# The state-space loop of a decoder kernel: one product with B in each pair of states moved from VectorE to GpSimd, by way of a copy made by ScalarE

## The chip, the cores and the metric

The kernel runs on one core of one Trainium2 chip. The metric is the device time of one execution in microseconds (us), as the median of several executions. Everything is computed in one launch: two decoder layers, six stages one after the other. The change touches one stage, the fourth.

## The reference

The reference is a two-layer decoder on 1024 tokens of width 128. The part that matters is the mixer of the second layer, a selective state-space scan over 1024 tokens with 256 channels (`Din`) and N = 16 states:

```python
dbc = u @ x_proj_w
dt, Bm, Cm = dbc[..., :dt_rank], dbc[..., dt_rank:dt_rank + N], dbc[..., dt_rank + N:]
delta = jax.nn.softplus(dt @ dt_proj_w + dt_proj_b)
A = -jnp.exp(A_log)
dA = jnp.exp(delta[..., None] * A)
dBu = delta[..., None] * Bm[:, :, None, :] * u[..., None]
def step(h, xs):
    dA_t, dBu_t, C_t = xs
    h = dA_t * h + dBu_t
    y = jnp.einsum('bdn,bn->bd', h, C_t)
    return (h, y)
```

So for each state n and each channel: a decay `exp(-a*delta)`, a drive `du * B[n]` with `du = delta * u`, a scan over the tokens, and a read `h * C[n]` that is summed over the states.

## The kernel before

The stages run one after the other; between two stages all engines meet and GpSimd clears the semaphores of the stage that ended (line 2807). The state-space stage is `mamba_stage`. Channels lie on the 128 partitions in two halves (`CH` = 2, index `j`), tokens along the free dimension, so that every large tile is 128x1024 float32. After a preparation that computes `delta` and `du`, each engine runs its own loop over pairs of states, `Fori(0, STATES // 2) as m`, with `s` = 0, 1 for the two states of a pair and `j` = 0, 1 for the two halves: 16 states, 32 (state, half) steps. There is no planner; the order on each engine is the order of its program, and semaphores join them.

- **ScalarE** (lines 1693 to 1701): for each (s, j) it waits until the scan before it is done (`scanned`) and writes the decay into the PSUM tile `B[1]` (line 1697). There is only one decay tile. After both halves it waits for TensorE's `c_mm` and copies the row of C, spread over all partitions, from `B[0]` into `c_rows[s]` (line 1701).
- **TensorE** (lines 1749 to 1788): `spread` multiplies with selector matrices so that one row of B or C stands on all 128 partitions, always in the PSUM tile `B[0]`; two matmuls of 512 columns. `B[0]` serves B and C in turn: the row of C is spread when both drives of the state are done (`spread_c`, line 1766 waits on `driven`), and the next row of B when C has been copied out (`spread_b`, line 1770 waits on `c_copied`). `add_reads` (eight matmul records in a row) adds the two read products of a state into `B[2]` and `B[3]`. In `next_state(n)` the order is: C of state n + 1, B of state n + 2, reads of state n.
- **VectorE** (lines 1872 to 1882): for each (s, j) the drive `du * B[0]` into the tile `drive[:, j, :]` (line 1877), and then the scan, which reads the decay in `B[1]` and the drive (line 1881).
- **GpSimd** (lines 1648 to 1655): the read product `state * c_rows` of each (s, j) (line 1654), after `c_copied` and the scan.

The four lines of VectorE that set the pattern:

```python
V.tensor_tensor(drive[:, j, :], du[:, j, :], B[0][:], ALU.mult).then_inc(S["driven"], 1)
e.wait_ge(S["driven"], 4 * m + (2 * s + j + 1 + DRIVEN0))
e.wait_ge(S["decayed"], 4 * m + (2 * s + j + 1))
V.tensor_tensor_scan(state[:, s, j, :], B[1][:], drive[:, j, :], 0.0, ALU.mult, ALU.add)
```

After the loop VectorE adds the skip term when all reads are summed (`y_all`), gates, and TensorE makes the output projection.

## Time and profile before

| what | value |
|---|---|
| median of 3 runs | 2874.75 us (2874.26 to 2877.35) |
| the profiled execution, its own time | 2881.46 us |
| its span, first to last instruction | 2879.5 us |
| busy over the span: PE, DVE, ACT, POOL | 84%, 75%, 53%, 11% |
| mean granted TensorE clock | 0.906 |
| the loop of the state-space stage, first to last scan | 1453.72 to 1569.72 us |

PE is TensorE, DVE VectorE, ACT ScalarE, POOL GpSimd, SP the queue of SyncE. The page divides the span into slices and gives for each engine the busy share; the loop lies in slices 21 and 22 of 40, the only ones behind the first stage in which GpSimd is much used. The shares of the whole span say little about one loop of 116 us: the timeline of that stretch, in which every instruction has its start, its length, and what ended the idle time before it, says which engine waits for which. In a timeline neighbouring instructions of one form are merged (x2, x8), and the idle time in brackets is that of the engine before the row.

### The profile page before, as it was taken

The page shows a single profiled execution, that of the slowest core. Times are in us where ns is not written, and L with a number is a line of the kernel's source. Part 1 is how long each engine was busy: PE and PEld are TensorE (multiplying, and loading weights), DVE is VectorE, ACT ScalarE, POOL GpSimd, SP SyncE. Part 2 cuts the span into 40 slices and gives each one's busy share as a digit, 9 for nine tenths or more (in the row PEclk, how much of TensorE's full clock was granted, in tenths as well). Part 3 has the DMA queues.
Part 4 walks back from the last instruction along what each step waited for, and adds up shares of the span by engine and source line. Part 5 has one row for each costly group of instructions (what it writes and reads, how often), then busy time and mean ns, then how long its engine had stood idle before and what let it go on. Part 6 is the DMA issues. An engine that isn't in the chain of part 4 may idle for free. (4 is left out here: it accounts for less than half of the span.)

```text
span 2879.5 us, 35672 instructions
## 1 busy us (share of the span) xinstructions
PE 2431.1 (84%) x10344; PEld 894.0 (31%) x10344; DVE 2149.5 (75%) x3171; ACT 1538.8 (53%) x1852; POOL 327.6 (11%) x333
## 2 busy tenths in 40 slices
PE   5888725799999987999657479999999999995997
PEld 3555401122222213444212213333333333332443
DVE  6777748899999204444498689999999999966665
ACT  4544417576767872333343457666676666652111
POOL 5655620000000000000045000000000000000000
PEclk8988855799999997999879679999999999997999
DMA  3433469100000105777200522013013110112000
GB/s 95 135 113 120 141 119 119 26 27 24 24 24 24 30 25 136 192 191 190 56 1 0 125 57 61 28 43 88 26 32 98 31 30 28 32 35 101 0 0 7
DMA packets 186315, 189.65 MB, mean 66 GB/s; under 512 B 18542, under 2 KB 158259, under 8 KB 184909
## 3 DMA queue, kind: packets, MB, share of 16 engines
...
## 5 line engine op out<-in xcount | busy, mean ns | idle before, releaser
L2459 DVE TENSOR_TENSOR y_acc<-y_acc,y_probs 128x1024 f32<-128x1024 f32 x408 | 496.7, 1217 | 33.9 <-ACT y_probs L2155 23.7
L2155 ACT ACTIVATE y_probs<-y_E,y_mask_bias 128x1024 f32<-128x1024 f32 x416 | 441.5, 1112 | 67.6 <-PE y_E L2240 59.2
L1080 ACT ACTIVATE x_probs<-x_E 128x1024 f32<-128x1024 f32 x408 | 397.2, 1023 | 138.0 <-PE x_E L1137 135.6
L1245 DVE TENSOR_REDUCE x_maxima<-x_M 128x1 f32<-128x496 f32 x676 | 420.5, 669 | 26.7 <-PE x_M L1119 15.4
L2249 PE MATMUL y_O<-y_probs,y_values 128*64 128x512 f32 x1664 | 402.8, 605 | 0.0
L2239 PE MATMUL y_E<-y_qa,y_ks 128*128 128x512 f16 x832 | 319.9, 385 | 1.2 <-ACT y_copied L2131 1.2
L2240 PE MATMUL y_E<-y_qb,y_ks 66*128 66x512 f16 x832 | 318.3, 383 | 0.0
L2131 ACT ACTIVATE y_copied<-y_M 128x1024 bf16<-128x1024 f32 x164 | 168.1, 1025 | 209.5 <-PE y_M L2206 209.5
L2397 DVE TENSOR_REDUCE y_maxima<-y_M 128x2 f32<-128x1024 f32 (+1 forms) x195 | 239.0, 1225 | 37.2 <-PE y_M L2206 25.2
L1566 DVE TENSOR_TENSOR f_hidden<-f_act_out,f_spread 128x512 f32<-128x512 f32 x160 | 110.6, 692 | 171.2 <-ACT f_act_out L1450 163.3
L1137 PE MATMUL x_E<-x_qs,x_keys 128*128 128x512 bf16 x816 | 220.8, 385 | 4.6 <-ACT x_probs L1080 2.9
L1150 PE MATMUL x_O<-x_probs,x_values 128*32 128x512 f32 x1632 | 218.0, 606 | 0.6 <-ACT x_probs L1080 0.6
L1450 ACT ACTIVATE f_act_out<-f_b 128x512 f32<-128x512 f32 x160 | 95.5, 598 | 186.6 <-PE f_b L1482 186.6
L2206 PE MATMUL y_M<-y_ks,y_qa 64*128 64x512 f16 x742 | 148.9, 398 | 26.4 <-DVE y_maxima L2397 23.6
L1487 PE MATMUL f_b<-f_hidden,f_weights 128*128 128x512 f32 x320 | 165.0, 598 | 5.3 <-DVE f_hidden L1566 5.3
L1482 PE MATMUL f_b<-f_xnT,f_weights 128*128 128x512 f32 x320 | 165.7, 600 | 1.1 <-ACT f_act_out L1450 1.1
L1119 PE MATMUL x_M<-x_keys,x_qs 64*128 64x496 bf16 x338 | 136.7, 404 | 23.8 <-DVE x_maxima L1245 23.4
L2249 PEld LDWEIGHTS y_O<-y_probs,y_values 128*64 128x64 f32 x1664 | 101.7, 136 | 171.8 <-issue 156.2
L2665 PE MATMUL g_b<-g_w_in,g_xT 128*128 128x512 f32 x256 | 119.6, 609 | 23.7 <-ACT g_xT L2625 16.4
L1119 PE MATMUL x_M<-x_keys,x_qm 64*128 64x496 bf16 x338 | 136.8, 405 | 0.0
L2408 DVE TENSOR_TENSOR y_running<-y_running,y_copied 128x1024 bf16<-128x1024 bf16 x192 | 131.7, 686 | 3.9 <-ACT y_copied L2131 3.4
L2239 PEld LDWEIGHTS y_E<-y_qa,y_ks 128*128 128x128 f16 x832 | 81.6, 98 | 141.6 <-issue 45.8
...
## 6 DMA issues: line engine op xcount, KB each, us to landing
...
```

Of the source, the lines that this page charges most:

```text
L1080: nc.scalar.activation(probs[:, n % 2, 2 * g:2 * g + 2, :], psE[:, 2 * g:2 * g + 2, :], ACT.Exp).then_inc(exped, 1)
L1119: T.matmul(banks[j], q, ks[r, 4 * (u // 2) + 2 * h + j, CHUNK0 * c:CHUNK0 * c + CHUNK0], start=True, stop=True).then_inc(done, 1)
L1137: ins = T.matmul(psE[:, j, :], ks[:, 4 * (u // 2) + j, P * t:P * t + P], qs[:, u, j, :], start=True, stop=True)
L1150: ins = T.matmul(psO[32 * j:32 * j + 32, :], values[:, i, 32 * j:32 * j + 32], probs[:, n % 2, j, :], start=(t == 0), stop=(t == TILES0 - ...
L1245: V.tensor_reduce(maxima[:, 2 * h + j, qt, c:c + 1], psM[(2 * entry + j) % 3][:, 0:CHUNK0], AX.X, ALU.max).then_inc(max_done, 1)
L2131: A(out, scores, ACT.Copy).then_inc(S["spare_copied"], 1)
L2155: A(probs[:, i, :], psE[:, 2 * (i % 2):2 * (i % 2) + 2, :].rearrange("p a b -> p (a b)"), ACT.Exp, bias=mask_bias[:, bass.ds(c * TILES_IN_ ...
L2239: T.matmul(psE[:, 2 * slot + j, :], ks1[:, u // 2 % 2, keys], qa[:, u, j, :], start=True, stop=False)
L2240: ins = T.matmul(psE[:, 2 * slot + j, :], ks2[:, u // 2 % 2, keys], qb[:, u, j, :], start=False, stop=True)
L2249: ins = T.matmul(psO[u % 2][DH1 * j:DH1 * j + DH1, :], values[:, i, DH1 * j:DH1 * j + DH1], probs[:, i, 512 * j:512 * j + 512], start=Fals ...
L2397: V.tensor_reduce(maxima[:, u % 2, :, 2 * g, bass.ds(c, 1)], psO_pair[:] if (u, g) == (0, 1) else psM[:], AX.X, ALU.max)\
L2459: ins = V.tensor_tensor(acc[:, u % 2, :], acc[:, u % 2, :], probs[:, i, :], ALU.add)
```

## The change

GpSimd makes the drive of (s, j) = (1, 1), one of the four of a pair of states, in a tile `pool_drive`; VectorE makes the other three. GpSimd reads B from a new tile `b_rows` in SBUF, which ScalarE copies from `B[0]` once in each pair, at the start of s = 1 and ahead of the decays of that state. GpSimd makes its product between the reads (0, 0) and (0, 1). VectorE's drive (1, 0), which reads `B[0]` as the copy does, waits for `b_copied`. TensorE's `spread_c` counts three drives in a pair, and for s = 1 it waits for the one drive that VectorE makes of that state and for `b_copied`. There are two new semaphores. In full:

```diff
--- before.py
+++ after.py
@@ -1612,10 +1612,11 @@
         drive = sb("drive", [P, CH, TOKENS])
         state, read = sb("state", [P, 2, CH, TOKENS]), sb("read", [P, 2, CH, TOKENS])
         c_rows = sb("c_rows", [P, 2, TOKENS])
+        b_rows, pool_drive = sb("b_rows", [P, TOKENS]), sb("pool_drive", [P, TOKENS])
 
         names = ("load load_in load_sel consts dve to_pow from_pow scaled_in bias_mm biased xn tr xT xz copied conv_done "
                  "silu_done dbc_mm dbc_done reduced split stacked dt_mm z_done neg exped one lned inved soft driver a_exp "
-                 "a_done b_mm c_mm c_copied decayed driven scanned was_read y_mm y_all gated out_mm added").split()
+                 "a_done b_copied pool_driven b_mm c_mm c_copied decayed driven scanned was_read y_mm y_all gated out_mm added").split()
         S = {n: sem(n) for n in names}
         LOADS_IN, LOADS = 3, 8
 
@@ -1647,8 +1648,13 @@
                 nc.gpsimd.memset(upad[:, :, 0:TAPS - 1], 0.0).then_inc(S["consts"], 1)
                 with e.Fori(0, STATES // 2) as m:
                     for s in range(2):
-                        e.wait_ge(S["c_copied"], 2 * m + (s + 1 + C0))
                         for j in range(CH):
+                            if (s, j) == (0, 1):
+                                e.wait_ge(S["b_copied"], m + 1)
+                                e.wait_ge(S["scanned"], 4 * m + SCAN0)
+                                nc.gpsimd.tensor_tensor(pool_drive[:], du[:, 1, :], b_rows[:], ALU.mult)\
+                                    .then_inc(S["pool_driven"], 1)
+                            e.wait_ge(S["c_copied"], 2 * m + (s + 1 + C0))
                             e.wait_ge(S["scanned"], 4 * m + (2 * s + j + 1 + SCAN0))
                             e.wait_ge(S["y_mm"], 4 * m + (2 * s + j - 3 + Y0))
                             nc.gpsimd.tensor_tensor(read[:, s, j, :], state[:, s, j, :], c_rows[:, s, :], ALU.mult)\
@@ -1690,8 +1696,13 @@
                     A(du[:, j, :], delta[:, j, :], ACT.Exp, scale=-1.0).then_inc(S["inved"], 1)
                 e.wait_ge(S["soft"], CH)
                 e.sem_inc(S["c_copied"], C0)
+                e.sem_inc(S["pool_driven"], DRIVEN0)
                 with e.Fori(0, STATES // 2) as m:
                     for s in range(2):
+                        if s == 1:
+                            e.wait_ge(S["b_mm"], 2 * m + 2)
+                            e.wait_ge(S["pool_driven"], m + DRIVEN0)
+                            A(b_rows[:], B[0][:], ACT.Copy).then_inc(S["b_copied"], 1)
                         for j in range(CH):
                             e.wait_ge(S["scanned"], 4 * m + (2 * s + j + SCAN0))
                             A(B[1][:], delta[:, j, :], ACT.Exp,
@@ -1762,28 +1773,30 @@
                                            skip_group_check=True)
                         ins.then_inc(S["y_all"] if last else S["y_mm"], 1)
 
-                def spread_c(n):
-                    e.wait_ge(S["driven"], 2 * n + (2 + DRIVEN0))
-                    spread(0, n + STATES).then_inc(S["c_mm"], 1)
+                def spread_c(m, s):
+                    e.wait_ge(S["driven"], 3 * m + (2 + s))
+                    if s:
+                        e.wait_ge(S["b_copied"], m + 1)
+                    spread(0, 2 * m + (s + STATES)).then_inc(S["c_mm"], 1)
 
                 def spread_b(n):
                     e.wait_ge(S["c_copied"], n + C0)
                     spread(0, n).then_inc(S["b_mm"], 1)
 
-                def next_state(n, s, first=False):
-                    spread_c(n + 1)
-                    spread_b(n + 2)
-                    add_reads(n, s, first)
+                def next_state(m, s, first=False):
+                    spread_c(m if s == 0 else m + 1, 1 - s)
+                    spread_b(2 * m + (s + 2))
+                    add_reads(2 * m + s, s, first)
 
                 spread(0, 0).then_inc(S["b_mm"], 1)
-                spread_c(0)
+                spread_c(0, 0)
                 spread_b(1)
                 next_state(0, 0, first=True)
-                next_state(1, 1)
+                next_state(0, 1)
                 with e.Fori(1, STATES // 2 - 1) as m:
                     for s in range(2):
-                        next_state(2 * m + s, s)
-                spread_c(STATES - 1)
+                        next_state(m, s)
+                spread_c(STATES // 2 - 1, 1)
                 add_reads(STATES - 2, 0)
                 add_reads(STATES - 1, 1, last=True)
                 for h in range(2):
@@ -1798,7 +1811,7 @@
             def _(e):
                 V = nc.vector
                 step = Steps(e, S["dve"])
-                for name, start in (("driven", DRIVEN0), ("was_read", READ0), ("y_mm", Y0), ("scanned", SCAN0)):
+                for name, start in (("was_read", READ0), ("y_mm", Y0), ("scanned", SCAN0)):
                     e.sem_inc(S[name], start)
                 norm_statistics(nc, step, x, stats, moments, 1e-5, var[:]).then_inc(S["to_pow"], 1)
                 V.tensor_scalar(neg_ident[:], ident[0:PROJ, 0:PROJ], -1.0, None, ALU.mult)
@@ -1873,12 +1886,18 @@
                     for s in range(2):
                         e.wait_ge(S["b_mm"], 2 * m + (s + 1))
                         for j in range(CH):
+                            source = pool_drive[:] if (s, j) == (1, 1) else drive[:, j, :]
                             e.wait_ge(S["scanned"], 4 * m + (2 * s + j - 1 + SCAN0))
-                            V.tensor_tensor(drive[:, j, :], du[:, j, :], B[0][:], ALU.mult).then_inc(S["driven"], 1)
-                            e.wait_ge(S["driven"], 4 * m + (2 * s + j + 1 + DRIVEN0))
+                            if (s, j) == (1, 1):
+                                e.wait_ge(S["pool_driven"], m + (1 + DRIVEN0))
+                            else:
+                                if s:
+                                    e.wait_ge(S["b_copied"], m + 1)
+                                V.tensor_tensor(source, du[:, j, :], B[0][:], ALU.mult).then_inc(S["driven"], 1)
+                                e.wait_ge(S["driven"], 3 * m + (2 * s + j + 1))
                             e.wait_ge(S["decayed"], 4 * m + (2 * s + j + 1))
                             e.wait_ge(S["was_read"], 4 * m + (2 * s + j - 3 + READ0))
-                            V.tensor_tensor_scan(state[:, s, j, :], B[1][:], drive[:, j, :], 0.0, ALU.mult,
+                            V.tensor_tensor_scan(state[:, s, j, :], B[1][:], source, 0.0, ALU.mult,
                                                  ALU.add).then_inc(S["scanned"], 1)
                 for j in range(CH):
                     e.wait_ge(S["y_all"], j + 1)
```

## Rows read from the trace of the kernel before

**Rows 1.** Groups, state-space loop and end: line, form, count; busy us, mean ns; idle, releasers.

```profile
L1654 POOL TENSOR_TENSOR ssm_read<-ssm_state,ssm_c_rows 128x1024 f32<-128x1024 f32 x32 | 74.6, 2355 | 94.9 <-ACT ssm_c_rows L1701 91.4 <-DVE ssm_state L1881 3.5
L1881 DVE TENSOR_TENSOR_SCAN ssm_state<-m_b,ssm_drive 128x1024 f32<-128x1024 f32 x32 | 73.3, 2291 | 4.2 <-DVE ssm_drive L1877 3.6
...
L1877 DVE TENSOR_TENSOR ssm_drive<-ssm_du,m_b 128x1024 f32<-128x1024 f32 x31 | 37.5, 1208 | 4.7 <-PE m_b L1752 4.2
L1697 ACT ACTIVATE m_b<-ssm_delta,ssm_a_neg 128x1024 f32<-128x1024 f32 x31 | 34.7, 1120 | 56.1 <-DVE ssm_state L1881 56.1
...
L1701 ACT ACTIVATE ssm_c_rows<-m_b 128x1024 f32<-128x1024 f32 x16 | 16.4, 1025 | 11.8 <-PE m_b L1752 11.8
```

**Rows 2.** First and last scan of the loop, timeline: start us, length us, instruction.

```profile
1453.72 2.29 DVE L1881 TENSOR_TENSOR_SCAN ssm_state<-m_b,ssm_drive 128x1024 f32<-128x1024 f32 x1
...
1569.72 2.29 DVE L1881 TENSOR_TENSOR_SCAN ssm_state<-m_b,ssm_drive 128x1024 f32<-128x1024 f32 x1 [0.23 <-DVE ssm_drive L1877]
```

**Rows 3.** Timeline, all engines, 1485 to 1493 us (x2, x8: merged instructions).

```profile
1485.12 2.29 DVE L1881 TENSOR_TENSOR_SCAN ssm_state<-m_b,ssm_drive 128x1024 f32<-128x1024 f32 x1
...
1487.33 1.20 DVE L1877 TENSOR_TENSOR ssm_drive<-ssm_du,m_b 128x1024 f32<-128x1024 f32 x1
...
1487.55 1.12 ACT L1697 ACTIVATE m_b<-ssm_delta,ssm_a_neg 128x1024 f32<-128x1024 f32 x1 [3.06 <-DVE ssm_state L1881]
...
1488.68 0.60 PE L1752 MATMUL m_b<-ssm_stack,ssm_sel 120*128 120x512 bf16 x2 [0.26 <-DVE ssm_drive L1877]
1488.75 2.29 DVE L1881 TENSOR_TENSOR_SCAN ssm_state<-m_b,ssm_drive 128x1024 f32<-128x1024 f32 x1 [0.23 <-DVE ssm_drive L1877]
1489.32 1.02 ACT L1701 ACTIVATE ssm_c_rows<-m_b 128x1024 f32<-128x1024 f32 x1 [0.66 <-PE m_b L1752]
...
1490.50 0.60 PE L1752 MATMUL m_b<-ssm_stack,ssm_sel 120*128 120x512 bf16 x2 [1.21 <-ACT ssm_c_rows L1701]
1490.59 4.66 POOL L1654 TENSOR_TENSOR ssm_read<-ssm_state,ssm_c_rows 128x1024 f32<-128x1024 f32 x2 [3.17 <-ACT ssm_c_rows L1701]
...
1491.14 1.22 DVE L1877 TENSOR_TENSOR ssm_drive<-ssm_du,m_b 128x1024 f32<-128x1024 f32 x1
1491.17 1.12 ACT L1697 ACTIVATE m_b<-ssm_delta,ssm_a_neg 128x1024 f32<-128x1024 f32 x1 [0.82 <-DVE ssm_state L1881]
...
1492.39 2.29 DVE L1881 TENSOR_TENSOR_SCAN ssm_state<-m_b,ssm_drive 128x1024 f32<-128x1024 f32 x1
```

**Rows 4.** Timeline, the first change of state, 1457 to 1462 us.

```profile
1457.36 2.29 DVE L1881 TENSOR_TENSOR_SCAN ssm_state<-m_b,ssm_drive 128x1024 f32<-128x1024 f32 x1 [0.24 <-DVE ssm_drive L1877]
1458.25 1.02 ACT L1701 ACTIVATE ssm_c_rows<-m_b 128x1024 f32<-128x1024 f32 x1 [0.98 <-PE m_b L1752]
...
1459.33 1.04 PE L1752 MATMUL m_b<-ssm_stack,ssm_sel 120*128 120x512 bf16 x2 [1.12 <-ACT ssm_c_rows L1701]
...
1460.41 1.22 DVE L1877 TENSOR_TENSOR ssm_drive<-ssm_du,m_b 128x1024 f32<-128x1024 f32 x1 [0.75 <-PE m_b L1752]
1461.66 2.29 DVE L1881 TENSOR_TENSOR_SCAN ssm_state<-m_b,ssm_drive 128x1024 f32<-128x1024 f32 x1
```

**Rows 5.** Timeline, two scans with a turn of the loop between them.

```profile
1496.02 2.29 DVE L1881 TENSOR_TENSOR_SCAN ssm_state<-m_b,ssm_drive 128x1024 f32<-128x1024 f32 x1 [0.23 <-DVE ssm_drive L1877]
...
1499.75 2.29 DVE L1881 TENSOR_TENSOR_SCAN ssm_state<-m_b,ssm_drive 128x1024 f32<-128x1024 f32 x1
```

**Rows 6.** Timeline, TensorE at two later places of the loop.

```profile
1505.56 3.60 PE L1760 MATMUL m_b<-ssm_read,ident_sb 128*128 128x512 f32 x8
...
1520.19 5.29 PE L1760 MATMUL m_b<-ssm_read,ident_sb 128*128 128x512 f32 x8
```

**Rows 7.** Windows, one row for the whole loop: us, busy times (counts), PEclk, DMA share.

```profile
1453.72:1569.72 116.00, 75.97 (x172) 28.36 (x173) 107.13 (x63) 50.09 (x46) 69.99 (x30) 0.86 0.00 0
```

**Rows 8.** Timeline, last two read products on GpSimd.

```profile
1571.62 4.65 POOL L1654 TENSOR_TENSOR ssm_read<-ssm_state,ssm_c_rows 128x1024 f32<-128x1024 f32 x2 [2.68 <-ACT ssm_c_rows L1701]
```

**Rows 9.** One line (L2807): duration min/median/max in ns, first and last start.

```profile
L2807 POOLq EVENT_SEMAPHORE_RANGE_CLEAR  x272: 44/44/48, 367.6 to 2875.5; - x136
```

## The prediction

> **What bounds the kernel now.** The change touches one loop, and the stages follow one another with all engines meeting in between, so I read that loop first and carry its difference to the end unchanged. Its stretch by the first and the last scan is 116.00 us [rows 2]; over it VectorE is busy for 107.13 us, with no DMA share behind it [rows 7]. By the groups view VectorE holds 32 scans of 2.29 us and 32 drives of 1.21 us, and ScalarE has 56.1 us of idle time ahead of its decays, all of it ended by a scan [rows 1]. Busy at 92%, VectorE looks like the bound, and a product taken from it would be worth 1.2 us. The timeline corrects that.
>
> Within a state [rows 3]: a scan starts at 1485.12, the next drive runs from 1487.33 to 1488.53, and the next scan starts only at 1488.75. What it waited for is the decay: there is one decay tile, which the running scan reads, so ScalarE starts the next decay at 1487.55, after the scan, and ends it at 1488.67. Scan, 0.14 to 0.22 of hand-over, decay 1.12, 0.08 of hand-over: 3.63 us from scan to scan, and the drive of 1.20 lies in its shadow with 0.22 to spare. The view puts that idle time down to the drive, which had long been done.
>
> Between two states [rows 3], counted from the scan start at 1488.75: C is spread until +0.53, copied by ScalarE from +0.57 to +1.59, B is spread from +1.75 to +2.35, the drive starts at +2.39 and the scan at +3.64. The next decay runs from +2.42 to +3.54. Both chains end together, so a crossing at the higher TensorE clock costs as much as a step within a state. At the lower clock the spread takes 1.04 instead of 0.60 and the crossing 4.30 [rows 4]. Where the loop turns it is 3.73 [rows 5].
>
> **The product that leaves VectorE** is the drive of (1, 1). It stands behind scan (1, 0), inside a state, where the decay chain gives 3.63 with or without it. Removed: 8 x 1.21 = 9.7 us of busy time, worth 0 us; what hides it is ScalarE's decay. If the decay did not need the scan's end it would be worth 1.2 each.
>
> **GpSimd's product** has no row of its own. The nearest is the read product, the same operation on the same shape in SBUF: 2.36 us [rows 1]. From scan (0, 1) as zero: read (0, 0) from 1.84 to 4.20 [rows 3], the new product to 6.55, read (0, 1) to 8.9. It waits for `b_copied` (3.41 below) without loss. It is needed for scan (1, 1) at 8.4, so it is covered by 1.8 us. Read (0, 1), queued behind it, is late by 2.4 us; it feeds `add_reads`, which TensorE comes to only after B of the next pair at about 10.1. GpSimd holds five products, 11.8 us, in a pair of some 15.6. Cost 0; below zero is excluded, since nobody gains from it, and above it is a rival.
>
> **The copy of B** is the term that counts. It has the form of the C copy, 1.02 us [rows 1, 3]. Counted from scan (0, 1): B is spread at +2.35, the copy runs from +2.39 to +3.41. ScalarE's decay (1, 0), which started at +2.42, is queued behind it and ends at about +4.6. VectorE's drive (1, 0), which started at +2.39, now waits for the copy: start +3.50 with the 0.08 to 0.10 of hand-over that a scan has behind a decay, then 1.25 to the scan as in [rows 3]: +4.75. The crossing from s = 0 to s = 1 goes from 3.64 to 4.75, +1.11. At the lower clock the same steps give 5.41 from 4.30 [rows 4]: +1.11 again. The bounds are 1.0 (no hand-over) and 1.25.
>
> A rule of the Trainium skill bears on that wait: PSUM — Partial Sum Buffer, "PSUM bank collisions raise a hardware error", says that ScalarE and VectorE must not read one bank at the same time. By that rule the copy cannot lie beside the drive. If it could, the drive would be free at +2.39, but the decay queued behind the copy would still hold the scan to about +4.65, so the sum would fall by 0.8 us in all. No row here shows such a collision.
>
> **The crossing from s = 1 to the next pair** gains. C of s = 1 now needs only the drive (1, 0), so it is spread early, and ScalarE copies it right behind decay (1, 1), from about 0 to +1.0 after scan (1, 1), instead of +0.57 to +1.59. B is then ready at +1.7 to +2.2, ahead of the scan's end even at the lower clock. The decay chain remains, 3.63, and at a turn of the loop perhaps 3.73 [rows 5]. Bounds 3.63 and 3.73; I take 3.68.
>
> **Sum for the loop.** Sixteen steps within a state at 3.63 are 58.1. Seven crossings to a next pair at 3.68 are 25.8. Eight crossings from s = 0 to s = 1: the first at the lower clock 5.4, the second still behind reads at the lower clock about 5.35, six at 4.75 are 28.5; together 39.3. That is 123.1, against 116.0 before: +7.1.
>
> **The clock.** Before, the mean granted clock over the loop is 0.86 [rows 7], a mix of the two levels of 1.2 and 2.4 GHz: the same eight read matmuls take 3.60 us or, partly at the lower level, 5.29 [rows 6]. TensorE's work per pair is unchanged, but its idle pieces grow: from C of s = 1, done at about +6.5, to B at +9.5 it now idles for 3 us, where it idled for 1.21 ahead of B before [rows 3]. A fall at the crossing from s = 0 to s = 1 costs 0.44 for B's spread and 0.44 for C's [rows 3, 4]. Bounds 0 and 0.88 x 6 = 5.3. I take a fall at three of the six, on one of the two spreads: 3 x 0.44 = +1.3, nearer to nothing because the trace of before is at the higher level for most of the loop.
>
> **The end.** The last C copy is 0.6 us earlier, and with it GpSimd's last two reads, 4.65 us, which wait for it [rows 8]: -0.6. Two more semaphores are cleared, 0.04 each [rows 9]: +0.1.
>
> Together 7.1 + 1.3 - 0.6 + 0.1 = **+7.9 us**. The profiled execution took 2881.46 us, 6.7 over the median of the runs shown; the difference is worked out within that execution (to 2889.4), and I apply it to the median: 2874.75 + 7.9 = **2882.6**.
>
> **The rivals.**
> *The gains eat the loss.* The terms at their low ends: crossings at 3.63 (-0.35), the hand-over at its shortest (-0.8), the second crossing at 4.75 (-0.6), no clock cost (-1.3): +4.9, or 2879.6, within 0.2%. For it: the 15 crossings of before take 116.0 - 58.1 = 57.9, or 3.86 each, 0.2 over the one in [rows 3], and that lateness can vanish. Against it: seven of them are already counted at 3.68. Chance 0.16.
> *TensorE falls behind.* With the clock low in a whole pair, the reads of the pair before, up to 7.2 us (twice 3.60 [rows 6]), run until about +10.1, C of s = 1 is spread after that, and the next crossing becomes 5.5 instead of 3.68; with 5.41 for the other one a low pair takes 2.5 us more than a high one. In half of the pairs: +10, so about 2891. For it the longer idle piece; against it that the reads right behind it keep TensorE busy. TensorE: Matmul & The Clock Gate, Part 1, in the Trainium skill, has the clock fall after idling and rise again under sustained work, which is this rival's mechanism. Chance 0.12.
> *Faster: VectorE's order is the bound.* If the hand-over of 0.22 ahead of scans were VectorE's own and the decay could run ahead, eight products of 1.21 would go and the copy would fill ScalarE's idle time: -9.7, or 2865. It decides from the point where a decay starts before the scan ahead of it ends; each decay in [rows 1, 3] starts behind a scan. Chance 0.04.
> *GpSimd is late*, or the change does not do what it says: the product would end after +8.4 if its reads were held up by 1.8 us; each microsecond beyond costs 8: about 2890. Chance 0.02.
> The forecast itself: 0.66.
>
> **Range and chances.** 0.2% is 5.7 us, about what a measurement of this kernel can tell from no change, so slower means above 2880.5. Slower: 0.66 + 0.12 + 0.02 = 0.80. Same 0.16, faster 0.04. The range reaches down past the first rival's 2879.6 to 2879.0, and up to 2890.0, the lower half of the second.
>
> **What the profile after would show.** Right: scans 3.63 apart within a state, also ahead of (1, 1), where VectorE idles for 1.3 us; 4.7 to 4.8 from (0, 1) to (1, 0), with the B copy, then decay and drive side by side in it; 3.63 to 3.73 into the next pair; GpSimd's product done about 1.8 us before its scan; the loop some 124 us from first to last scan. Wrong: scans less than 3.5 apart before (1, 1) (the decay was not the bound); a drive (1, 0) that starts beside the copy; scans (1, 1) released by GpSimd; or crossings into the next pair above 4 with TensorE still at its reads.

## The result and the profile after

The changed kernel took 2884.95 us in the median, against 2875.39 for the kernel before: ratio 1.0032, 95% interval 1.0020 to 1.0045, so between 5.8 and 12.9 us slower. With more executions of both (the first experiment) the ratio was 1.0023, 1.0013 to 1.0034. The forecast was +7.9 us, a ratio of 1.0027, inside both. The profiled execution spans 2880.0 us, only 0.5 over the one of before: executions of one program differ by several microseconds (2874.06 to 2877.35 in the six of before, 2881.64 to 2889.58 in the six of after), and here that spread hides what the loop lost. So I read the loop by itself, from its first to its last scan.

The groups view of the state-space stage after the change (line, engine, operation, tiles, count; busy us, mean ns of one; idle before, and what ended it), to be laid beside [rows 1]:

```profile
L1900 DVE TENSOR_TENSOR_SCAN ssm_state<-m_b,ssm_drive 128x1024 f32<-128x1024 f32 x24 | 55.0, 2290 | 3.7 <-DVE ssm_drive L1896 3.2 <-ACT m_b L1708 0.2
L1708 ACT ACTIVATE m_b<-ssm_delta,ssm_a_neg 128x1024 f32<-128x1024 f32 x32 | 35.7, 1116 | 59.0 <-DVE ssm_state L1900 53.3 <-DVE ssm_delta L1881 5.8
...
L1896 DVE TENSOR_TENSOR ssm_drive<-ssm_du,m_b 128x1024 f32<-128x1024 f32 x24 | 28.9, 1205 | 12.4 <-ACT ssm_b_rows L1705 12.1 <-DVE ssm_du L1883 0.3
...
L1655 POOL TENSOR_TENSOR ssm_pool_drive<-ssm_du,ssm_b_rows 128x1024 f32<-128x1024 f32 x8 | 18.8, 2355 | 0.0
L1900 DVE TENSOR_TENSOR_SCAN ssm_state<-m_b,ssm_pool_drive 128x1024 f32<-128x1024 f32 x8 | 18.3, 2291 | 10.7 <-POOL ssm_read L1660 5.4 <-ACT m_b L1708 5.4
...
L1705 ACT ACTIVATE ssm_b_rows<-m_b 128x1024 f32<-128x1024 f32 x8 | 8.2, 1024 | 8.9 <-PE m_b L1763 8.9
```

Eight of the 32 scans now take their drive from GpSimd, whose product lasts 2.36 us as its read products do. VectorE has 24 drives for 32, and in place of 4.7 us of idle time ahead of the drives it has 12.4, of which 12.1 are a wait for the copy of B. ScalarE has eight copies of 1.02 us more. The windows view of the loop, beside [rows 7]:

```profile
1451.92:1575.89 123.97, 81.88 (x178) 31.46 (x178) 97.45 (x55) 57.02 (x55) 88.38 (x38) 0.82 0.00 0
```

124.0 us instead of 116.0, VectorE busy for 97.45 instead of 107.13: the 9.7 us that left it, and nothing of them shows in the time. The mean granted clock of TensorE is 0.82 for 0.86. One pair of states in the timeline, to be read beside [rows 3]:

```profile
1487.31 0.60 PE L1763 MATMUL m_b<-ssm_stack,ssm_sel 120*128 120x512 bf16 x2 [2.14 <-DVE ssm_drive L1896]
1487.37 2.29 DVE L1900 TENSOR_TENSOR_SCAN ssm_state<-m_b,ssm_drive 128x1024 f32<-128x1024 f32 x1 [0.23 <-DVE ssm_drive L1896]
1487.95 1.02 ACT L1712 ACTIVATE ssm_c_rows<-m_b 128x1024 f32<-128x1024 f32 x1 [0.67 <-PE m_b L1763]
...
1489.12 0.60 PE L1763 MATMUL m_b<-ssm_stack,ssm_sel 120*128 120x512 bf16 x2 [1.21 <-ACT ssm_c_rows L1712]
...
1489.84 1.03 ACT L1705 ACTIVATE ssm_b_rows<-m_b 128x1024 f32<-128x1024 f32 x1 [0.87 <-PE m_b L1763]
...
1490.76 1.11 ACT L1708 ACTIVATE m_b<-ssm_delta,ssm_a_neg 128x1024 f32<-128x1024 f32 x1
1490.90 1.22 DVE L1896 TENSOR_TENSOR ssm_drive<-ssm_du,m_b 128x1024 f32<-128x1024 f32 x1 [1.24 <-ACT ssm_b_rows L1705]
...
1491.53 2.35 POOL L1655 TENSOR_TENSOR ssm_pool_drive<-ssm_du,ssm_b_rows 128x1024 f32<-128x1024 f32 x1
...
1492.16 2.29 DVE L1900 TENSOR_TENSOR_SCAN ssm_state<-m_b,ssm_drive 128x1024 f32<-128x1024 f32 x1
...
1494.59 1.12 ACT L1708 ACTIVATE m_b<-ssm_delta,ssm_a_neg 128x1024 f32<-128x1024 f32 x1 [2.71 <-DVE ssm_state L1900]
1494.69 0.60 PE L1763 MATMUL m_b<-ssm_stack,ssm_sel 120*128 120x512 bf16 x2
...
1495.64 1.00 ACT L1712 ACTIVATE ssm_c_rows<-m_b 128x1024 f32<-128x1024 f32 x1
1495.79 2.29 DVE L1900 TENSOR_TENSOR_SCAN ssm_state<-m_b,ssm_pool_drive 128x1024 f32<-128x1024 f32 x1 [1.34 <-ACT m_b L1708]
```

From scan (0, 1) at 1487.37: B is spread until 1489.72, ScalarE copies it from 1489.84, and only then starts the decay (1, 0) at 1490.76; VectorE's drive (1, 0) starts at 1490.90, behind the copy. Scan (1, 0) comes 4.79 after scan (0, 1), where it was 3.64. Then 3.63 to scan (1, 1), although VectorE stands idle for 1.34 of it, and 3.63 into the next pair (to 1499.42), with C copied right behind the decay (1, 1). GpSimd's product ended at 1493.88, 1.9 us before its scan.

All steps of the two profiles, from the starts of the 32 scans (my sums, in us):

| steps | before | after | after, again |
|---|---|---|---|
| 8 from (0, 0) to (0, 1), each | 3.63 | 3.63 | 3.63 |
| 8 from (0, 1) to (1, 0), sum | 30.6 | 40.5 | 39.8 |
| 8 from (1, 0) to (1, 1), sum | 29.0 | 29.1 | 29.1 |
| 7 into the next pair, sum | 27.4 | 25.4 | 25.4 |
| loop, first to last scan | 116.0 | 124.0 | 123.3 |
| last scan to the start of the next stage | 21.3 | 19.0 | 19.0 |

A remark on reading: at four of the eight scans (1, 1) the profile names a read of GpSimd as what ended the wait. The rows show why that is no bound:

```profile
1509.51 2.35 POOL L1660 TENSOR_TENSOR ssm_read<-ssm_state,ssm_c_rows 128x1024 f32<-128x1024 f32 x1
...
1510.69 1.12 ACT L1708 ACTIVATE m_b<-ssm_delta,ssm_a_neg 128x1024 f32<-128x1024 f32 x1 [2.71 <-DVE ssm_state L1900]
...
1511.89 2.29 DVE L1900 TENSOR_TENSOR_SCAN ssm_state<-m_b,ssm_pool_drive 128x1024 f32<-128x1024 f32 x1 [1.34 <-POOL ssm_read L1660]
```

The decay ends at 1511.81, the read at 1511.86, and the scan starts at 1511.89. The scan does not wait for that read (its wait on reads is for those of the pair before); it is only the last thing that ended. The step is 3.63 whichever of the two is named.

The crossings from (0, 1) to (1, 0) are not all 4.79. Two things lengthen them, and both come from TensorE's lower level. First, B's spread can take 1.03 us in place of 0.60: in four of the eight crossings of the first profile, the one from 1503.05 among them, that makes 5.21 of 4.79.

```profile
1504.80 1.03 PE L1763 MATMUL m_b<-ssm_stack,ssm_sel 120*128 120x512 bf16 x2 [1.21 <-ACT ssm_c_rows L1712]
```

Second, the eight reads of TensorE ahead of C's spread can take 5 to 6 us in place of 3.60, and C then comes late. In the second profile of the changed kernel reads of 6.17 us run from 1511.28, C is spread at 1517.29 in place of 1516.64, and the crossing from 1516.70 is 5.43, although both spreads took 0.60.

```profile
1511.28 6.17 PE L1771 MATMUL m_b<-ssm_read,ident_sb 128*128 128x512 f32 x8
```

These two marks, a spread of 1.03 and a C that is late behind long reads, are used for every kernel below.

### The profile page after: what moved, and what is told of

It reads as the page before. It is cut to its first block and busy times, and to the rows that moved or that the text cites. A ratio compares the mean times of both kernels' runs of the same rounds, so it can differ in the third digit from the quotient of the medians.

```text
span 2880.0 us, 35730 instructions
## 1 busy us (share of the span) xinstructions
PE 2431.4 (84%) x10344; PEld 896.9 (31%) x10344; DVE 2138.9 (74%) x3163; ACT 1544.5 (54%) x1860; POOL 345.0 (12%) x341
## 5 line engine op out<-in xcount | busy, mean ns | idle before, releaser
L2106 POOL TENSOR_TENSOR y_rstd<-y_var,mhalf 128x8 f32<-128x8 f32 x4 | 6.6, 1654 | 1032.8 <-DVE y_var L2497 1026.0
```

## The experiments

Each was judged first by the loop in its one profile and by the steps inside it, and then by its time. A step within a state is steady (3.62 to 3.65 us in every profile with one decay tile, but for the kernel that puts GpSimd's product behind both reads); the crossings vary with TensorE's clock, so the loops of two executions of one kernel differ too, by 0.7 us in the only pair taken (124.0 and 123.3). "Crossing" is the step from (0, 1) to (1, 0); the four labels of steps are those of the table above.

| kernel | loop | crossings, sum | (1, 0) to (1, 1), sum | into next pair, sum | ratio to before, 95% |
|---|---|---|---|---|---|
| before | 116.0 | 30.6 | 29.0 | 27.4 | |
| after, again | 123.3 | 39.8 | 29.1 | 25.4 | 1.0023 (1.0013 to 1.0034) |
| copy only | 129.8 | 40.3 | 29.1 | 31.4 | 1.0052 (1.0037 to 1.0066) |
| product only | 117.8 | 33.6 | 29.0 | 26.1 | 1.0002 (0.9993 to 1.0011) |
| copy later | 117.7 | 33.4 | 29.2 | 26.0 | 1.0001 (0.9991 to 1.0012) |
| two copies | 131.8 | 48.3 | 29.0 | 25.4 | 1.0054 (1.0036 to 1.0071) |
| product behind both reads | 125.9 | 40.5 | 30.9 | 25.4 | 1.0029 (1.0019 to 1.0040) |
| before, two decay tiles | 114.7 | 31.2 | 27.5 | 28.6 | 1.0004 (0.9995 to 1.0013) |
| after, two decay tiles | 123.0 | 44.2 | 17.7 | 33.7 | 1.0035 (1.0023 to 1.0047) |
| after, two zero matmuls | 129.5 | 46.0 | 29.1 | 25.4 | 1.0048 (1.0031 to 1.0064) |
| copy later, two zero matmuls | 118.3 | 34.7 | 29.2 | 25.4 | 1.0008 (0.9999 to 1.0017) |
| copy later, one zero matmul | 114.5 | 30.7 | 29.1 | 25.7 | 0.9993 (0.9983 to 1.0003) |
| before, one zero matmul | 117.7 | 30.9 | 29.0 | 28.8 | 1.0006 (0.9996 to 1.0016) |

**The changed kernel again**, with no edit.

> The changed kernel once more, unaltered, for a second profile and more executions. My theory: what the change costs lies in the loop alone, first to last scan 123.5 to 124.5 us against 116.0, so the median is 7 to 9 us over before; what differs by more between two profiles of other stages (the first profile of the changed kernel has its last scan 5 us nearer to the end than before) is not the change's and goes either way. The rival, that the change also moves other stages: the stretch from the last scan to the end again some 5 us shorter than in the trace of before.

Loop 123.3 us; the stretch from the last scan to the end 1303.4 us, as short as in the first profile of it (1304.1) and 6 us shorter than in the trace of before (1309.8). Over the profiles of all these kernels it lies between 1303.4 and 1309.8, and with the drives as they were before it is once 1304.6 (before, one zero matmul) and once 1309.6 (before, two decay tiles), so that most of this is likely the spread of executions and not the change. Two microseconds of it are the stage's own end, taken up below. The ratio of 1.0023 is +6.6 us, a little under the 7 to 9 I had written; the two intervals overlap between 1.0020 and 1.0034.

**Is it the copy or the product?** Copy only: GpSimd's product goes, VectorE makes all four drives.

```diff
...
-    source = pool_drive[:] if (s, j) == (1, 1) else drive[:, j, :]
+    source = drive[:, j, :]
...
-    if (s, j) == (1, 1):
-        e.wait_ge(S["pool_driven"], m + (1 + DRIVEN0))
-    else: ...
+    if s:
+        e.wait_ge(S["b_copied"], m + 1)
+    V.tensor_tensor(source, du[:, j, :], B[0][:], ALU.mult).then_inc(S["driven"], 1)
...
-    e.wait_ge(S["driven"], 3 * m + (2 + s))
+    e.wait_ge(S["driven"], 4 * m + (2 + 2 * s))
```

> ScalarE still copies B at the start of the second state, and the drive (1, 0) still waits for it, but VectorE makes all four drives and GpSimd none; the copy is read by nobody. My theory (the copy is the whole cost, the product was worth nothing): crossings from s = 0 to s = 1 of 4.6 to 5.4 us as in the changed kernel; the drive (1, 1) is back inside its 3.63; crossings into the next pair again 3.64 to 3.9 since C waits for the drive (1, 1). Loop 124 to 126 us, time 8 to 10 us over before. The rival that the product taken from VectorE is worth its 1.2 us and is eaten by the copy: loop 133 to 134. The rival that GpSimd's product costs something by itself: loop below 122.

The crossings sum to 40.3, as in the changed kernel: the copy and its wait make them by themselves. (The one from 1492.19, with both spreads at 0.60 and C on time, is 4.70; the last four are longer because C is spread 0.25 to 0.75 late.) The step (1, 0) to (1, 1) has its drive back on VectorE and is 3.63 all the same: the product taken away was worth nothing there. But the loop is 129.8 us and not 124 to 126, and my number was wrong: the crossings into the next pair sum to 31.4. One of them in the timeline:

```profile
1500.56 1.03 PE L1757 MATMUL m_b<-ssm_stack,ssm_sel 120*128 120x512 bf16 x2 [2.58 <-DVE ssm_drive L1887]
1501.63 1.02 ACT L1706 ACTIVATE ssm_c_rows<-m_b 128x1024 f32<-128x1024 f32 x1 [1.19 <-PE m_b L1757]
...
1502.81 1.03 PE L1757 MATMUL m_b<-ssm_stack,ssm_sel 120*128 120x512 bf16 x2 [1.22 <-ACT ssm_c_rows L1706]
...
1503.98 1.22 DVE L1887 TENSOR_TENSOR ssm_drive<-ssm_du,m_b 128x1024 f32<-128x1024 f32 x1 [1.16 <-PE m_b L1757]
...
1505.23 2.29 DVE L1891 TENSOR_TENSOR_SCAN ssm_state<-m_b,ssm_drive 128x1024 f32<-128x1024 f32 x1
```

Both spreads at the lower clock, 1.03 each, and with C waiting for the drive (1, 1) they lie on the path: 4.70 from scan to scan (1500.53 to 1505.23). So the change has a gain that I had taken as small: with the product on GpSimd C waits for one drive less, is spread early, and this crossing is out of the clock's reach at 3.63. Without it the loop would lose 6.0 us more (31.4 against 25.4). The mean clock of the loop fell to 0.77 in this run (window 1457 to 1570 us; before 0.87, after 0.83), so part of those 6 us is that clock. That the early C shields the crossing is seen in the kernel with two copies below: its mean clock in the same window is 0.77 as well, and its crossings into the next pair still sum to 25.4. By its time this kernel is slower than the changed one in the second measurement (1.0037 to 1.0066 against 1.0013 to 1.0034); against the first (1.0020 to 1.0045) the intervals overlap.

Product only: no copy of B; GpSimd multiplies with the row of C that is there, so that the sums are not the layer's, but every instruction keeps its shape. The waits for the copy go, and ScalarE's copy of C gets one wait more, for GpSimd's product of the pair before.

```diff
-    nc.gpsimd.tensor_tensor(pool_drive[:], du[:, 1, :], b_rows[:], ALU.mult)
+    nc.gpsimd.tensor_tensor(pool_drive[:], du[:, 1, :], c_rows[:, 0, :], ALU.mult)
...
-    A(b_rows[:], B[0][:], ACT.Copy).then_inc(S["b_copied"], 1)
...
+    if s == 0:
+        e.wait_ge(S["pool_driven"], m + DRIVEN0)
     A(c_rows[:, s, :], B[0][:], ACT.Copy).then_inc(S["c_copied"], 1)
...
```

> GpSimd makes the drive (1, 1), but no copy of B is made: it multiplies du with the row of C of s = 0 that is in SBUF anyway, so that this drive is du times C and not du times B. VectorE makes three drives. My theory: the product is worth nothing inside the decay chain, so steps within a state stay at 3.63, the crossing from s = 0 to s = 1 goes back to 3.64 (4.1 to 4.3 at the lower clock), and only the crossings into the next pair gain (3.63 for a mean of 3.9 before). Loop 112.6 to 115 us, time 1 to 4 us under before. The rival that the product is worth 1.2 us each: loop 106 to 107, time 10 us under before. The rival that the product on GpSimd costs: loop above 116.

Steps within a state 3.63 with one drive less: the product is worth nothing. But the loop is 117.8, above both the 112.6 to 115 I had expected and the 116.0 of before, since the crossings are 3.81 to 4.66 and not 3.64. By its number the rival that the product on GpSimd costs (loop above 116) has come, and the rows show two reasons, neither of them a wait for GpSimd:

```profile
1501.88 0.82 PE L1760 MATMUL m_b<-ssm_stack,ssm_sel 120*128 120x512 bf16 x2 [2.13 <-DVE ssm_drive L1889]
...
1503.99 1.03 PE L1760 MATMUL m_b<-ssm_stack,ssm_sel 120*128 120x512 bf16 x2 [1.29 <-ACT ssm_c_rows L1709]
...
1505.15 1.22 DVE L1889 TENSOR_TENSOR ssm_drive<-ssm_du,m_b 128x1024 f32<-128x1024 f32 x1 [0.91 <-PE m_b L1760]
...
1506.40 2.29 DVE L1893 TENSOR_TENSOR_SCAN ssm_state<-m_b,ssm_drive 128x1024 f32<-128x1024 f32 x1
```

C is spread in 0.82 and B in 1.03 instead of 0.60, and the drive waits for B until 1505.15. TensorE's clock has fallen again, with no copy in the kernel: B's spread took 1.03 in five of the eight crossings, where it took 1.03 or 1.04 in two before. What is new ahead of it is C's early spread and the longer idle piece behind it; that these are the cause is argued, not isolated. The other reason is not the clock: the two crossings with both spreads at 0.60 and C on time are 3.81 and 3.82, which is 0.18 over before. There C's copy, which has a wait more, starts 0.12 behind C's spread and not 0.04, and the drive 0.13 behind B's spread and not 0.04. The time is that of before (0.9993 to 1.0011), so the 1.8 us of the loop, one profile each, are not confirmed by it.

**Does the copy cost by its length or by its place?** Two copies:

```diff
+    A(en[:, 1, :], B[0][:], ACT.Copy)
     A(b_rows[:], B[0][:], ACT.Copy).then_inc(S["b_copied"], 1)
```

> The changed kernel with the suspected cost doubled: ScalarE copies B twice (first into a tile nobody reads, then into b_rows) before the decay (1, 0). My theory: each copy stands on the path once in a pair, so the crossing from s = 0 to s = 1 grows by 0.95 to 1.0 to about 5.8 (6.2 at the lower clock) and nothing else moves; loop 131 to 132.5 us, time 7 to 9 us over the changed kernel. The rival that the cost of the change is the wait or the clock and not the copy's length: loop within 3 us of 124.

Crossings 48.3 against 40.5, +7.8 us or 0.98 each; the other three kinds of steps did not move. Part of that is the clock: in the last six C is spread 0.16 to 0.47 late, as behind reads of 5.67 us at the crossing from 1487.12. With C's lateness taken off, these six are 5.70 each, 0.91 over 4.79, and the first two are 0.91 over those of the changed kernel (6.35 and 5.50 against 5.44 and 4.59). The second copy begins 0.92 after the first, and the drive waits for both:

```profile
1506.65 1.02 ACT L1705 ACTIVATE ssm_en<-m_b 128x1024 f32<-128x1024 f32 x1 [0.87 <-PE m_b L1764]
...
1507.57 1.02 ACT L1706 ACTIVATE ssm_b_rows<-m_b 128x1024 f32<-128x1024 f32 x1
...
1508.62 1.22 DVE L1897 TENSOR_TENSOR ssm_drive<-ssm_du,m_b 128x1024 f32<-128x1024 f32 x1 [2.47 <-ACT ssm_b_rows L1706]
```

So a copy ahead of this drive costs what it delays the drive, 0.91 us. The time has only two executions of this kernel behind it.

Copy later: ScalarE makes it behind the decay (1, 0) and the drive (1, 0), and that drive waits for nothing.

```diff
-    if s == 1:
-        e.wait_ge(S["b_mm"], 2 * m + 2)
-        e.wait_ge(S["pool_driven"], m + DRIVEN0)
-        A(b_rows[:], B[0][:], ACT.Copy).then_inc(S["b_copied"], 1)
     for j in range(CH):
+        if (s, j) == (1, 1):
+            e.wait_ge(S["driven"], 3 * m + 3)
+            e.wait_ge(S["pool_driven"], m + DRIVEN0)
+            A(b_rows[:], B[0][:], ACT.Copy).then_inc(S["b_copied"], 1)
...
-                                if s:
-                                    e.wait_ge(S["b_copied"], m + 1)
                                 V.tensor_tensor(source, du[:, j, :], B[0][:], ALU.mult).then_inc(S["driven"], 1)
```

> The changed kernel with the copy of B moved: ScalarE makes it behind the decay (1, 0) and when the drive (1, 0) is done, so neither the drive nor the decay (1, 0) waits for it. Everything is still computed. My theory (the place of the copy is the cost): the crossing from s = 0 to s = 1 goes back to 3.64 at the higher clock; GpSimd's product then starts at 4.9 and ends at 7.3 after scan (0, 1), just when scan (1, 1) could start (7.27), so that step becomes 3.7 to 3.9 and is released by GpSimd. Loop 114 to 117 us, time between 3 us under and 1 us over before, 6 to 10 under the changed kernel. The rival that any copy of 1.02 us on ScalarE costs its length, wherever it stands: loop 122 or more.

The loop is 117.7, 0.7 over my range and 6 us under the changed kernel. The time is that of before (1.0001), and its interval (0.9991 to 1.0012) lies under both intervals of the changed kernel (1.0020 to 1.0045 and 1.0013 to 1.0034): of all the runs this is the one that shows the cause by the time as well. The same copy of 1.02 us now costs nothing by itself:

```profile
1500.96 2.29 DVE L1898 TENSOR_TENSOR_SCAN ssm_state<-m_b,ssm_drive 128x1024 f32<-128x1024 f32 x1
1501.05 1.02 ACT L1706 ACTIVATE ssm_b_rows<-m_b 128x1024 f32<-128x1024 f32 x1 [0.71 <-DVE ssm_drive L1894]
...
1502.23 2.35 POOL L1655 TENSOR_TENSOR ssm_pool_drive<-ssm_du,ssm_b_rows 128x1024 f32<-128x1024 f32 x1 [1.23 <-ACT ssm_b_rows L1706]
...
1504.61 2.29 DVE L1898 TENSOR_TENSOR_SCAN ssm_state<-m_b,ssm_pool_drive 128x1024 f32<-128x1024 f32 x1 [1.36 <-POOL ssm_pool_drive L1655]
```

It runs beside scan (1, 0), GpSimd's product follows until 1504.58 and releases scan (1, 1) at 1504.61, 3.65 after scan (1, 0): 0.02 later than the decay would. So the place is the cost. The place means two things, and this edit takes both away: the drive (1, 0) no longer waits for the copy, and the decay (1, 0) no longer stands behind it on ScalarE. No run separates them. In the rows of the changed kernel above, the drive ended at 1492.12 and the decay at 1491.87, ahead of the scan at 1492.16, so the drive's wait was the longer of the two by about 0.2 us, and without it the decay alone would have kept most of the cost. What remains over 3.64 is the clock for the most part: six crossings are 4.16 to 4.59, and in all six B's spread took 1.03, in three of them C's 1.01 to 1.04 too. The crossings with both at 0.60 are 3.62 and 3.74; in the latter the drive starts 0.13 behind B's spread in place of 0.04, as it does in the run with no copy at all.

**Is GpSimd covered?** The product behind the read (0, 1), in GpSimd's program:

```diff
 for s in range(2):
     for j in range(CH):
-        if (s, j) == (0, 1): ...
-            nc.gpsimd.tensor_tensor(pool_drive[:], du[:, 1, :], b_rows[:], ALU.mult)
         nc.gpsimd.tensor_tensor(read[:, s, j, :], state[:, s, j, :], c_rows[:, s, :], ALU.mult)
+    if s == 0: ...
+        nc.gpsimd.tensor_tensor(pool_drive[:], du[:, 1, :], b_rows[:], ALU.mult)
```

> The changed kernel with GpSimd's product behind the read (0, 1) instead of ahead of it. My theory: GpSimd's product is covered by 1.8 us in the changed kernel; one read later it ends at 8.9 after scan (0, 1) where scan (1, 1) wants it at 8.4, so that step becomes 4.2 to 4.3 and is released by GpSimd: loop 128 to 129 us, time about 5 us over the changed kernel. At crossings at the lower clock (scan (1, 1) at 8.8) the step grows by 0.1 to 0.2 only. The rival that GpSimd has more slack than worked out: step (1, 1) still 3.63, loop 124.

```profile
1490.63 2.35 POOL L1660 TENSOR_TENSOR ssm_pool_drive<-ssm_du,ssm_b_rows 128x1024 f32<-128x1024 f32 x1
...
1493.01 2.29 DVE L1900 TENSOR_TENSOR_SCAN ssm_state<-m_b,ssm_pool_drive 128x1024 f32<-128x1024 f32 x1 [1.77 <-POOL ssm_pool_drive L1660]
```

In these rows the product ends at 1492.98 and the scan starts at 1493.01, 4.06 after scan (1, 0). Four of the eight steps grew, to 4.05 to 4.16, and the first, behind a crossing of 5.44, to 3.72; the three others behind crossings of 5.21 and more stayed at 3.63. The step is under the 4.2 to 4.3 that I had written: the product ended at 8.8 after scan (0, 1) and not at 8.9. The sum from scan (0, 1) to scan (1, 1) shows the bound: 8.84 here (1484.17 to 1493.01), so one read of 2.35 earlier the product was ready at 6.5, 1.9 us before its scan. The prediction had 1.8. Loop 125.9, under the 128 I wrote, since I had made all eight late. The time (1.0019 to 1.0040) does not tell this kernel from the changed one; the bound is shown by the rows alone.

**Is the decay chain the bound within a state?** Two decay tiles in the kernel before:

```diff
-    e.wait_ge(S["scanned"], 4 * m + (2 * s + j + SCAN0))
-    A(B[1][:], delta[:, j, :], ACT.Exp,
+    e.wait_ge(S["scanned"], 4 * m + (2 * s + j - 1 + SCAN0))
+    A((B[1][:], en[:, 1, :])[j], delta[:, j, :], ACT.Exp,
...
-    V.tensor_tensor_scan(state[:, s, j, :], B[1][:], drive[:, j, :], 0.0, ALU.mult,
+    V.tensor_tensor_scan(state[:, s, j, :], (B[1][:], en[:, 1, :])[j], drive[:, j, :], 0.0, ALU.mult,
```

> The kernel before with two decay tiles: the decay of j = 0 in the PSUM tile as now, that of j = 1 in an SBUF tile that is free by then, so that a decay no longer waits for the scan just ahead of it. My theory (the decay chain and the chain through the one tile of B and C end together at a crossing, the decay chain alone binds within a state): steps within a state fall from 3.63 to 3.45 to 3.5 where the drive and the scan on VectorE bind; crossings stay at 3.7 to 3.85 at the higher clock, now by the chain through the tile of B and C; loop 112.5 to 116 us, time 0 to 3 us under before. The rival that the decay chain isn't the bound within a state: steps still 3.63. A second rival by the Trainium skill (SBUF - State Buffer, SBUF: two separate sides): the scan of j = 1 now has two SBUF inputs, and such a VectorE instruction and a GpSimd one exclude each other; its read product starts 1.84 after that scan starts, so by the rule reads get late by up to 0.5 us with no effect on the loop.

```profile
1498.14 2.29 DVE L1881 TENSOR_TENSOR_SCAN ssm_state<-m_b,ssm_drive 128x1024 f32<-128x1024 f32 x1
...
1500.35 1.20 DVE L1877 TENSOR_TENSOR ssm_drive<-ssm_du,m_b 128x1024 f32<-128x1024 f32 x1
1501.57 2.29 DVE L1881 TENSOR_TENSOR_SCAN ssm_state<-ssm_en,ssm_drive 128x1024 f32<-128x1024 f32 x1
...
1505.40 2.29 DVE L1881 TENSOR_TENSOR_SCAN ssm_state<-m_b,ssm_drive 128x1024 f32<-128x1024 f32 x1
```

Within a state 3.43 (drive, and the scan 0.02 behind it), at crossings 3.83 and, at a turn of the loop, 3.92 or more: the decay was the bound within a state, and B's and C's common tile takes over at the crossing, as worked out. A state has gained 0.2 and lost 0.2; loop 114.7, time unchanged. Of the rival with the two SBUF inputs the trace shows as much as was expected: the 16 scans from `ssm_en` keep their 2.29, and a read that begins while one of them runs gets longer, up to 2.52 for 2.35, without effect on the loop.

The same lines edited in the changed kernel, where the product should now count:

> The changed kernel with the same two decay tiles. Here the product taken from VectorE should at last be worth something: scan (1, 1) has its decay early and its drive from GpSimd at 6.5 after scan (0, 1), so it follows scan (1, 0) directly. My theory: step (1, 0) to (1, 1) 2.3 to 2.5 instead of 3.63, the crossing from s = 0 to s = 1 still 4.75 to 5.2 by the copy, the crossing into the next pair 3.5 to 3.65: loop 109 to 113 us, time 4 to 7 us under before. The rival that the product is worth nothing even then: step still above 3.4. The second rival, by the Trainium skill (SBUF - State Buffer, SBUF: two separate sides), is that the scan (1, 1), now with two SBUF inputs, is held off by GpSimd's read (0, 1), which runs from 6.5 to 8.9: step 4.0 to 4.3, loop 122 to 125.

Missed. Scan (1, 1) starts 2.21 after scan (1, 0), as it should, and yet the loop is 123.0 and not 109 to 113. That is the loop of the second rival (122 to 125), though not its step (4.0 to 4.3). The tile view of the states shows where it went (min/median/max in ns):

```profile
L1660 POOL TENSOR_TENSOR ssm_read<-ssm_state,ssm_c_rows x32: 2337/2352/4352, 1456.3 to 1579.2; 128x1024 f32<-128x1024 f32 x32
...
L1900 DVE TENSOR_TENSOR_SCAN ssm_state<-ssm_en,ssm_drive x8: 2290/2291/2291, 1454.0 to 1565.9; 128x1024 f32<-128x1024 f32 x8
L1900 DVE TENSOR_TENSOR_SCAN ssm_state<-ssm_en,ssm_pool_drive x8: 3536/3591/4221, 1461.8 to 1573.5; 128x1024 f32<-128x1024 f32 x8
```

The scan with both inputs in SBUF takes 2.29 us eight times and 3.54 to 4.22 the other eight, and a read of GpSimd up to 4.35 instead of 2.35. The timeline shows the two at one time:

```profile
1509.08 2.34 POOL L1660 TENSOR_TENSOR ssm_read<-ssm_state,ssm_c_rows 128x1024 f32<-128x1024 f32 x1
...
1510.03 3.54 DVE L1900 TENSOR_TENSOR_SCAN ssm_state<-ssm_en,ssm_pool_drive 128x1024 f32<-128x1024 f32 x1
```

The read began first and ends at 1511.42; the scan, recorded from 1510.03, ends at 1513.57, 2.15 after it. That is 0.14 less than a whole scan of 2.29, as if it had stood nearly at its beginning until GpSimd was through. It goes the other way as well: the next two reads, begun at 1512.21 under that scan, take 5.83 together, where two take 4.65 elsewhere. The Trainium skill (SBUF — State Buffer, "SBUF: two separate sides") has this as an exclusive lock: a VectorE instruction with two SBUF inputs and a GpSimd one that reads SBUF exclude each other, and whichever starts first holds it for its whole length. The trace agrees, in both orders, with the instruction's length and not its start as the place where it shows. None of the scans and drives of the kernels before and after has two SBUF inputs, which is why their scans keep their 2.29 beside GpSimd. The steps into the next pair went up to 4.7 and more, since they begin with that long scan. The crossings went up too, to a sum of 44.2; in four of them both spreads took 1.03, at a mean clock of 0.80 from 1457 to 1570 us.

**Is the rest the clock?** Matmuls with a tile of zeros, which GpSimd clears once ahead of the loop, are added to the sums of the reads and fill TensorE's idle piece behind the reads of s = 0:

```diff
+zero = sb("zero", [P, 512])
...
+nc.gpsimd.memset(zero[:], 0.0).then_inc(S["zeroed"], 1)
...
     add_reads(2 * m + s, s, first)
+    if s == 0:
+        fill()
...
+def fill():
+    for b in range(2):
+        T.matmul(B[2 + b][:, 0:512], ident[:], zero[:], start=False, stop=False, skip_group_check=True)
+
+e.wait_ge(S["zeroed"], 1)
```

> The changed kernel with two matmuls of a zero tile (512 columns each, added to the sums of the reads, which they leave as they are) behind the reads of s = 0 in each pair, to fill TensorE's idle piece ahead of C's spread at the crossing from s = 0 to s = 1. My theory: the part of that crossing over 4.79 us (5.21 to 5.44 in most pairs of the two profiles) is the spreads of C and B at the lower clock after an idle piece; filled, at least six of the eight crossings are 4.75 to 4.85, the mean clock of the loop rises from 0.83 to over 0.9, loop 122 to 123 us, time 1 to 2 us under the changed kernel. The rival that the idle piece has nothing to do with it: crossings and clock as in the changed kernel. A second: the added work comes late at the lower clock and delays C: crossings above 5.5.

The second rival it was: crossings of 5.4 to 6.6 in seven of eight.

```profile
1519.42 1.88 PE L1797 MATMUL m_b<-ssm_zero,ident_sb 128*128 128x512 f32 x4
...
1520.31 2.29 DVE L1909 TENSOR_TENSOR_SCAN ssm_state<-m_b,ssm_drive 128x1024 f32<-128x1024 f32 x1 [0.23 <-DVE ssm_drive L1905]
...
1521.14 0.60 PE L1765 MATMUL m_b<-ssm_stack,ssm_sel 120*128 120x512 bf16 x2
...
1525.98 2.29 DVE L1909 TENSOR_TENSOR_SCAN ssm_state<-m_b,ssm_drive 128x1024 f32<-128x1024 f32 x1
```

The filling ran until 1521.30, and C, due 0.07 ahead of the scan at 1520.31 as elsewhere, is recorded at 1521.14; the crossing is 5.67. The filling did not reach the other idle piece, ahead of B's spread (3.21 us in this trace); behind it the clock was low, the reads took 4.7 to 5.8 in six of seven pairs and not 3.60, and the filling came too late. The filling itself took 1.88 each time, and both spreads of these late crossings took 0.60: by then the clock was up again. Behind the one set of reads that took 3.60 the crossing is 4.79.

The same addition to the kernel with the copy later:

> The kernel with the copy of B moved behind the drive (1, 0), with the same two zero matmuls. My theory: its crossings from s = 0 to s = 1, 3.62 to 4.59 with a sum of 33.4, fall to about 3.65 each (29 to 30), loop 113.5 to 115 us, 1 to 2 us under the kernel before, which is then the best of the versions. The rival that the zero matmuls stand in C's way there, since a pair is only 14.6 us long: crossings of 4 and more, loop 117 or more.

Four of eight crossings at 3.74, the first at 4.38, and three of 4.8 to 5.7: 118.3. The three are those behind reads of 5.3 to 6.0 us; behind reads of 3.60 all are 3.74. So the filling is harmless when the reads ahead of it ran at the higher level, and in the way when they did not.

One matmul instead of two:

```diff
-        for b in range(2):
+        for b in range(1):
```

> The same with one zero matmul instead of two: half of the idle piece (0.9 of 1.85 us) is filled. My theory: the clock still falls now and then; sum of the crossings from s = 0 to s = 1 between 30 and 33, loop 114 to 117 us. If the filling is what counts, it lies between the version with two and the one with none; if two stand in C's way, this one is the best of the three.

Loop 114.5, the shortest of all, with six crossings of 3.63 to 3.74, one of 3.95, and the first, at the lower clock, of 4.39. The windows view from 1457 to 1570 us, for the version without filling and this one (the last columns are the granted clock and the DMA share and rate):

```profile
1457.00:1570.00 113.00, 80.80 (x178) 31.45 (x178) 92.78 (x51) 55.48 (x52) 87.58 (x38) 0.85 0.00 0
```

```profile
1457.00:1570.00 113.00, 81.92 (x195) 32.43 (x196) 93.74 (x52) 55.47 (x52) 90.52 (x40) 0.92 0.00 0
```

The clock rises from 0.85 to 0.92 and the crossings fall from 33.4 to 30.7: in this pair of profiles 2.7 of the 4.3 us by which the crossings exceeded 8 x 3.64 went with the clock. A higher mean clock is not enough, though: the version with two zero matmuls has 0.90 in the same window and a loop of 118.3. One profile each, and the ratio, 0.9993 with an interval that holds 1, doesn't tell this kernel from the one before. The first crossing has both spreads at the lower clock in every version.

And one in the kernel before, behind the reads of every state:

```diff
     add_reads(n, s, first)
+    fill()
...
+    for b in range(1):
+        T.matmul(B[2 + b][:, 0:512], ident[:], zero[:], start=False, stop=False, skip_group_check=True)
...
```

> The kernel before with one zero matmul behind the reads of each state. My theory: half a microsecond of TensorE's idle piece of 1.45 us remains, the clock stays at its higher level once it is there, crossings 3.64 and 3.73 except the first three: loop 113.5 to 115 us for 116.0, time 1 to 2 us under before, hard to tell in the medians. So the lateness of crossings that the prediction found in before, 0.2 us each, is the clock's too. The rival that it is not: loop 116.

Missed: 117.7. The crossings from s = 0 are 3.64 or 3.65 in six of eight, as expected, but three others are 4.70 to 4.77, where the filling stood in C's way (at one, reads that took 5.29 from 1547.86, the filling at 1553.00, and C 0.9 late at 1553.86). Two more, 4.30 and 4.41, are the first two of the loop, with both spreads at 1.03 as in the kernel before. So the sum does not show that the lateness of before was the clock's. The trace of before does: of its 15 crossings of both kinds nine are 3.64 to 3.74, and each of the six longer ones (3.85 to 4.40) has one of the two marks. In four a spread took 1.03 or 1.04; in two C came 0.1 and 0.4 late behind reads of 5.29 and 5.77 us.

## Why the prediction was right

- **The bound.** Right. Within a state it is scan, decay, scan: 3.63 with the drive on VectorE, with the drive on GpSimd, and 3.43 only when the decay got a second tile, with the drive on VectorE then the bound. VectorE's 92% were not a bound.
- **The product worth nothing.** Right for the step it stood in: 29.0 before, 29.1 after, 29.1 with the copy alone. Its whole worth is in the crossing into the next pair, below.
- **GpSimd's product at 2.36, covered by 1.8 us.** Right: 2.36, 1.9.
- **The copy, +1.11 at a crossing.** Right: 4.79 in the timeline above for 4.75, so 8 x 1.1, and a second copy added 0.91 each with C's lateness taken off.
- **Crossings into the next pair at 3.68.** 3.63 each, 25.4 for 25.8. That is a gain of 2.0 us on the 27.4 of before, where my 25.8 made 1.6 of it. The run with the copy alone shows that it is worth more in a kernel that has been slowed: 6 us at its clock. The step itself, that C is spread early, was read rightly; what it shields from was mis-sized.
- **The clock, +1.3.** The crossings summed to 40.5 and 39.8, where 39.3 + 1.3 had been worked out: right in size, and partly by luck. In the first profile the second crossing was 4.59 and not 5.35 (-0.8), B's spread was at the lower level in four of the last six and not three (+1.7 for +1.3), and the six began from 4.79 and not 4.75 (+0.2). In the second profile both spreads took 0.60 in all of the last six; instead the reads ran long once and made C late (+0.65). So the amount was near and what makes it up differs from one execution to the next. I had drawn the fall from the idle piece behind C's early spread; the run with the product alone shows it without the copy, where B's spread fell in five of eight, but that the idle piece is its cause stays argued.
- **The rivals.** TensorE fell behind, but not where that rival had it: in the second profile C waited for reads at two crossings from s = 0 (5.02 and 5.43), and nowhere did this touch the crossing into the next pair. Of the rival in which gains eat the loss two of four terms came, the 3.63 and the short second crossing; the hand-over and the clock did not. VectorE's order was not the bound, and GpSimd was not late.
- **The end, -0.6.** Mis-sized. From the last scan to the next stage it is 19.0 for 21.3, so -2.3. GpSimd's last reads begin 1.07 after the last scan, where they began 1.90 after it [rows 8]:

```profile
1576.96 4.65 POOL L1660 TENSOR_TENSOR ssm_read<-ssm_state,ssm_c_rows 128x1024 f32<-128x1024 f32 x2 [1.12 <-ACT ssm_c_rows L1712]
...
1586.27 3.84 PE L1806 MATMUL m_b<-ssm_out_proj,ssm_conv 128*128 128x128 f32 x32 [2.63 <-DVE ssm_conv L1909]
```

That is -0.8. The rest, 1.5, is the output projection, 3.84 us here and 5.47 in the trace of before, at the lower clock there; over all profiles here both values occur with either order of the C copy (3.84 in seven, 5.2 to 5.5 in the other seven), so it is the clock of the moment and not the change. From the first scan to the next stage the two profiles of the changed kernel are +5.6 and +5.0 us over before, and the two measured ratios stand for +6.6 and +9.2. The forecast of +7.9 lies between these; which of its last two microseconds are the change's, the runs do not settle. That it falls inside both intervals is more than its terms can claim: the loop alone differed by 0.7 us between two executions of the changed kernel, and of before there is one profile.
